# A twelve-layer latent transformer on one core: range clears, a key norm on two engines, early weights, and a new order of transfers in the 16-head layers

## What is computed

```python
x = x + L0_xattn(ctx, ln(x))   # 8 heads, ctx normalised row by row, rotary keys
x = x + L0_attn(ln(x));  x = x + L0_ffn(ln(x))
x = x + L1_xattn(ln(x), ctx)   # 16 heads of 16, mask per key
x = x + L1_attn(ln(x));  x = x + L1_ffn(ln(x))
x = x + L2_xattn(ln(x), ctx)   # 8 heads, cosine and variance terms
x = x + L2_attn(ln(x));  x = x + L2_ffn(ln(x))
x = x + L3_xattn(ln(x), ctx)   # 16 heads of 16, mask per query and key
x = x + L3_attn(ln(x));  x = x + L3_ffn(ln(x))
```

## Time and profile before

| | |
|---|---|
| median of 3 runs | 2720.01 us (2719.88 to 2721.12) |
| the profiled execution | 2719.54 us, its span 2717.6 us |
| mean granted clock of TensorE | 0.932 |
| busy: PE, PEld, DVE, ACT, POOL | 2356.9, 1462.9, 1794.6, 1238.8, 519.2 us |
| instructions | 58520 |

### The profile page before, as it was taken

The page is one execution under the profiler, slowest core; times in us unless marked ns, Lnnn a source line. Parts: engine busy times, 40 slices in busy tenths (PEclk is TensorE's granted clock), DMA queues, the critical chain, the costliest instruction groups (busy, mean ns, idle before and its releaser), DMA issues. The chain is left out here.

```text
span 2717.6 us, 58520 instructions
## 1 busy us (share of the span) xinstructions
PE 2356.9 (87%) x22114; PEld 1462.9 (54%) x22116; DVE 1794.6 (66%) x2945; ACT 1238.8 (46%) x2102; POOL 519.2 (19%) x297
## 2 busy tenths in 40 slices
PE   4699997999996585999997989999997449999978
PEld 3444434666564572666665745555555425555548
DVE  6466666888887617666662277777776767777721
ACT  6655554333332533777774233333332305555542
POOL 0255552000000002000000036555552010000000
PEclk8799998999998796999998999999998669999989
DMA  7677784565662448676673322222221057667554
GB/s 252 245 244 246 245 278 136 163 182 176 171 191 72 166 158 199 166 171 150 167 156 127 138 79 95 95 95 95 95 81 61 33 127 166 150 158 157 141 138 172
DMA packets 255993, 416.92 MB, mean 153 GB/s; under 512 B 32333, under 2 KB 217202, under 8 KB 255702
## 3 DMA queue, kind: packets, MB, share of 16 engines
q1 hardware_dynamic: 246902, 412.33, 52.4%
q10 hardware_dynamic: 8928, 2.23, 0.6%
HBM read 323.65 MB, written 90.85 MB: 153 GB/s over the span
## 5 line engine op out<-in xcount | busy, mean ns | idle before, releaser
L1493 DVE CUSTOM_DVE_ANT_0 l1x_junk<-l1x_pm,l1x_mrow,l1x_top 128x896 bf16<-128x896 f32 x224 | 247.1, 1148 | 112.7 <-PE l1x_pm L1649 112.6
L1493 DVE CUSTOM_DVE_ANT_0 l3x_junk<-l3x_pm,l3x_mrow,l3x_top 128x896 bf16<-128x896 f32 x224 | 246.1, 1147 | 88.7 <-PE l3x_pm L1649 88.2
L1577 ACT ACTIVATE l1x_prob<-l1x_ring,mask_col 128x512 f32<-128x512 f32 x392 | 248.1, 685 | 115.3 <-PE l1x_ring L1669 114.1
L1580 ACT ACTIVATE l3x_prob<-l3x_ring 128x512 f32<-128x512 f32 x392 | 213.2, 595 | 161.2 <-PE l3x_ring L1673 161.2
L2438 ACT ACTIVATE l2x_fsq<-l2x_f 128x1024 f32<-128x1024 f32 x98 | 103.5, 1057 | 276.6 <-DVE l2x_f L2326 276.6
L1068 ACT ACTIVATE l0x_att_pt<-l0x_att_pt 128x1024 f32<-128x1024 f32 x99 | 104.7, 1058 | 262.0 <-DVE l0x_att_pt L1007 262.0
L2610 POOL TENSOR_TENSOR l2x_gk<-l2x_f,l2x_ks 128x1024 f32<-128x1024 f32 x98 | 184.4, 1919 | 158.1 <-DVEq L2351 158.1
L1112 PE MATMUL l0x_att_pv<-l0x_wv,l0x_att_vin 128*128 128x512 f32 x392 | 194.4, 618 | 1.3 <-DVE l0x_att_tops L995 1.3
L2483 PE MATMUL l2x_kf<-l2w_w,l2x_nin 128*128 128x512 f32 x392 | 171.8, 598 | 4.3 <-DVE l2x_f L2326 3.8
L2483 PE MATMUL l2x_kf<-l2w_w,l2w_first 128*128 128x512 f32 x392 | 171.3, 597 | 0.0
L2326 DVE TENSOR_TENSOR l2x_f<-l2x_kf,l2w_bias 128x1024 f32<-128x1024 f32 x98 | 120.0, 1224 | 76.0 <-PE l2x_kf L2483 63.6
(11 more groups left out here) (695 smaller groups left out, 4836.3 us busy)
## 6 DMA issues: line engine op xcount, KB each, us to landing
l1x_kt<-scratch_KS SPq DMA_DIRECT2D x84, 448.0 KB, 9.2
l3x_kt<-scratch_KS SPq DMA_DIRECT2D x84, 448.0 KB, 8.8
scratch_KT<-l0x_max_kf SPq DMA_DIRECT2D x28, 896.0 KB, 7.0
l0x_att_kt<-scratch_KT SPq DMA_DIRECT2D x56, 448.0 KB, 7.1
scratch_KS<-l0x_side_kp SPq DMA_DIRECT2D x14, 1344.0 KB, 13.8
scratch_KS<-l2x_side_kp SPq DMA_DIRECT2D x14, 1344.0 KB, 5.8
l0fw_w<-L_ffn_exp_w SPq DMA_DIRECT2D x16, 1024.0 KB, 7.8
l1fw_w<-L_ffn_W SPq DMA_DIRECT2D x16, 1024.0 KB, 8.8
```

The costliest lines, as they stand in the source:

```text
L1493: dve.tensor_tensor_reduce(junk[x % 2][:, :, :], pm[x % 2][:, :, 0:SPLIT], mrow[b][:, :].rearrange("p (s k) -> p s k", s=2), 1.0, top[1 - ...
L1577: ins = act.activation(into, scores, ACT.Exp, bias=R.mask_col[:, bass.ds(m * TILES + n // 4, 1)])
L1580: ins = act.activation(into, scores, ACT.Exp)
```

## The change

- Semaphores are cleared by ranges of neighbouring numbers, dealt to SP, GpSimd, ScalarE and VectorE.
- Of the seven tiles of a chunk ScalarE scales five and VectorE two (tensor_scalar), in `factors`. In l0x chunk 0's statistics stand ahead of the wait for the vectors, and the pieces of other work move by one or two chunks.
- `AheadWeights` holds w_in of l0a and of l2a and all weights of l3a in a Stage of their own; they are loaded at the ends of l0x and l2x, and in l3x before the loop, and closed after l0f, l2a and l3f.
- In l1x and l3x the stack is loaded after the parts are in DRAM, and the values before. ScalarE loads only the first buffer of rows; the second is copied from the first by SP (`second_copy`). Two of the four query copies are on ScalarE, and TensorE begins after the first half.
- The spread, the products and the copy of `FoldedKeys` move from l1f to l1a; the scaling stays in l1f.

```diff
@@ Stage.__exit__
-            engines = (self.nc.gpsimd, self.nc.sync, self.nc.scalar, self.nc.vector, self.nc.tensor)
-            for n, s in enumerate(self.sems.values()):
-                engines[n % len(engines)].sem_clear(s)
+            engines = (self.nc.sync, self.nc.gpsimd, self.nc.scalar, self.nc.vector)
+            for n, numbers in enumerate(runs_of(s.num for s in self.sems.values())):
+                engines[n % len(engines)].sem_clear(numbers)
             self.nc.all_engine_barrier()
@@ KeyNorm.factors (DVE); scale (ACT) runs over range(self.BY_SCALAR), BY_SCALAR = 5
+        if m >= 2:
+            dve.wait_ge(self.sem("turned"), DC * (m - 1))
+        for t in range(self.BY_SCALAR, TILES):
+            last = dve.tensor_scalar(self.xn[m % 2][:, t, :], self.raw[m % self.DEPTH][:, t, :],
+                                     self.mv[m % 2][:, t, 0:1], self.rs[m % 2][:, t:t + 1], ALU.subtract, ALU.mult)
+        last.then_inc(self.sem("scaled_last"), 1)
@@ QueryRows
-        for rows in self.rows:
-            parts_to_rows(act, rows, self.scratch, PARTS_OF_Q, self.S.sem("q_in"))
+        parts_to_rows(act, self.rows[0], self.scratch, PARTS_OF_Q, self.S.sem("q_in"))
+    def second_copy(self, sp):
+        self.wait(sp)
+        sp.dma_start(self.rows[1][0:STACK], self.rows[0][0:STACK]).then_inc(self.S.sem("q_again"), 16)
@@ Heads16.run, SP
                     lead.sync(sp)
                     sp.wait_ge(S.sem("q_out"), 16)
+                    self.load_stack(sp, 0, 0)
+                    self.ones_rows(sp)
                     lead.later_sync(sp)
-                    self.ones_rows(sp)
+                    q.second_copy(sp)
                     top_to_rows(0, 0)
                     lead.last_sync(sp)
@@ Heads16.run, PE
-                    pe.wait_ge(S.sem("queries"), 1)
+                    pe.wait_ge(S.sem("queries"), 2)
                     for x in range(units):
+                        if x == units // 2:
+                            pe.wait_ge(S.sem("masked_q"), 2)
+                            pe.wait_ge(S.sem("queries_last"), 2)
                         max_unit(0, 0, x)
...
                     q.wait(pe)
+                    q.wait_second(pe)
@@ l1x Lead
-                heads.load_stack(sp, 0, 0)
+                self.late(sp.dma_start(w[:, 1, :, :], by_rows(A["L1_xattn_wv"])))
+                self.late(sp.dma_start(bv[:, :], A["L1_xattn_bv"].partition_broadcast(P)))
+                heads.load_values(sp, 0, 0)
@@ l3x Lead
-                heads.load_stack(sp, 0, 0)
+                heads.load_values(sp, 0, 0)
...
                 def last_sync(self, sp):
-                    pass
+                    R.ahead.load(sp)
@@ both Leads: masked_queries on DVE, turned_queries at the end of scalar
+        if c == 0:
+            dve.wait_ge(S.sem("masked_q"), 1)
+            dve.tensor_copy(qb_turned[c][0:64, :, :], qb[c][64:P, :, :]).then_inc(S.sem("queries"), 1)
+            dve.tensor_copy(qb_turned[c][64:P, :, :], qb[c][0:64, :, :]).then_inc(S.sem("queries"), 1)
+    act.wait_ge(S.sem("masked_q"), 2)
+    act.activation(qb_turned[1][0:64, :, :], qb[1][64:P, :, :], ACT.Copy).then_inc(S.sem("queries_last"), 1)
+    act.activation(qb_turned[1][64:P, :, :], qb[1][0:64, :, :], ACT.Copy).then_inc(S.sem("queries_last"), 1)
@@ l0a, l2a, PE (l3a the same)
-                pe.wait_ge(S.sem("w_in"), 16)
+                R.ahead.wait(pe)
@@ l1a, PE, after the last product of po and before the turn of xn
+                R.folded.tensor(pe, pa[:, 0:2, :])
                 turn_tensor(pe, S, "o", xn, pt, R.ident, ready="gated")
@@ l1f, PE
-                F.tensor(pe, ph[1])
                 turn_tensor(pe, S, "n", xn, pt, R.ident)
```

More of the change, by code:

```diff
@@ L31, with runs_of @@
 MASK_HEAD = MASK_ROW // 16
+def runs_of(numbers):
+    runs = []
+    for n in sorted(numbers):
+        if runs and runs[-1].stop == n:
+            runs[-1] = range(runs[-1].start, n + 1)
+        else:
+            runs.append(range(n, n + 1))
+    return runs
 class Stage:
@@ L259, in output, with __init__, load, tensors @@
         last.then_inc(S.sem("y"), 1)
+class AheadWeights:
+    def __init__(self, nc, name, parts):
+        self.S = Stage(nc, name)
+        self.buffers = [(self.S.sb(key, shape), pieces) for key, shape, pieces in parts]
+        self.loads = Loads(self.S.sem("loads"))
+    def load(self, sp):
+        for buffer, pieces in self.buffers:
+            for at, src in pieces:
+                self.loads(sp.dma_start(buffer[at], src))
+    def tensors(self):
+        return [buffer for buffer, _ in self.buffers]
+    def wait(self, eng):
+        eng.wait_ge(self.S.sem("loads"), self.loads.total)
+    def close(self):
+        self.S.__exit__(None, None, None)
 def l3_attn(nc, A, R):
@@ L274, in l3_attn @@
         pt, pqk, pv = S.psum("pt"), S.psum("pqk"), S.psum("pv")
-        loads = Loads(S.sem("weights"))
         block = S.nc.Block()
@@ L291, in _ @@
                 turn_vector(dve, S, "n", xT, pt)
-                dve.wait_ge(S.sem("weights"), loads.total)
+                R.ahead.wait(dve)
                 dve.wait_ge(S.sem("projected"), 1)
@@ L1945, in l0_xattn @@
     INNER = H * HD
+    R.ahead = AheadWeights(nc, "l0aw", [("w_in", [P, DC, 1024], [(slice(None), by_rows(A["L0_attn_W_in"]))])])
     with Stage(nc, "l0x") as S:
@@ L2191, in l2_xattn @@
     w, bias = folded.w, folded.bias
+    R.ahead = AheadWeights(nc, "l2aw", [("w_in", [P, DC, 1024], [(slice(None), by_rows(A["L2_attn_W_in"]))])])
     with Stage(nc, "l2x") as S:
@@ L2663, in mamba @@
     with Stage(nc, name) as S:
-        w_in = S.sb("w_in", [P, DC, 2 * INNER])
+        w_in, = R.ahead.tensors()
         w_out = S.sb("w_out", [P, IC, DIM])
@@ L2850, in l2_attn @@
                             "conv_b": "L2_attn_b_conv", "A_log": "L2_attn_A_log", "D": "L2_attn_D"}, True)
+    R.ahead.close()
+    R.folded.S.__exit__(None, None, None)
 class DecayWeights:
```

98 lines of the change are left out of this document (53 added, 45 removed).

## The result

The changed kernel takes **2707.68 us** (median of 5 runs, 2704.32 to 2710.64) against 2720.11 for the kernel before, run beside it (5 runs, 2719.88 to 2725.06). The ratio is 0.9946, 95% interval 0.9935 to 0.9957. It is faster, but by 12.4 us and not by 31: outside the range of the forecast.

A forecast was written before the change was run, and what follows sets the result against it. Twelve layers run one after the other, TensorE busy 87% of the span but waiting at their starts and ends. Gains 8.6 + 10.5 + 6.3 + 0.8 + 5.0 = 31.2 from 2719.5 give 2688.3, median 2689 us; range 2678 to 2700.

The forecast's parts named there:

- A: At the stage exits: clearing semaphores by range, with none on TensorE, gains 8.6 us (range 3 to 9.6).
- The other bound: At the stage exits: a clear might cost by its width, 0.05 us for each of some 470 semaphores.
- B and C: In l0x: earlier first statistics and the key norm split between ScalarE and VectorE gain 10.5 us (range 4 to 12.5).
- D: In l0a, l2a and l3a: first weights loaded a stage early gain 6.3 us (range 4 to 8).
- E: Folded pieces moved from l1f into TensorE's idle time in l1a gain 0.8 us (range -2 to 1.5).
- F: At the starts of l1x and l3x: new transfer order and shared query copies gain 5.0 us (range -2 to 12.4).
- the change does not do what it says: Rival, 0.08: in l1x and l3x the parts cross a queue that is not empty; l1x gains 0, l3x -3; 2696 us.
- Transfers share instead of queueing: Rival, 0.17: high parts move beside the stack and land in time; l1x gains 11.1, l3x 1.4; 2681 us.
- the forecast's own case: Main case, 0.53: 2683 to 2693 us; in l1x and l3x the high parts land behind stack and row loads.
- The slower rival, SP's serial chain: Rival, 0.04: in l1x and l3x parts, rows, second copy and tops follow each other; 18.8 us slower, 2738 us.

The follow-up runs named there:

- fourth: The changed kernel with all seven tiles of a chunk scaled by ScalarE again, l0x's earlier start kept: 2710.07 us, ratio 0.9962.
- fifth: The changed kernel with VectorE's piece of bias work in l0x one chunk later (m == 8, not 7): 2702.59 us, ratio 0.9928.
- third kernel: The kernel before the change with nothing but the semaphore clears by range: 2712.49 us, ratio 0.9973.
- seventh: The changed kernel with the second copy issued behind the first tops, and only the second chunk waiting for it: 2707.41 us, ratio 0.9939.
- ninth: The changed kernel, l1x and l3x first transfers issued without SP's wait, high parts and mask before stack, l0x bias work a chunk later: 2684.25 us.
- eleventh: The changed kernel with the folded pieces (spread, eight products, copy) back in l1f: 2709.85 us, ratio 0.9952.
- tenth: The changed kernel with six row loads of 256-byte pieces replaced by two of 4 KB pieces, same bytes, rows in wrong order: 2702.55 us.

## Why the prediction was right in sign and wrong in size

**A was right.** Forecast 8.6, the exits show 8.8, the clears alone 7.9 in the whole time. The other bound, a clear that costs 0.05 us for each semaphore, is excluded: the longest of the 53 took 0.28 us, the median 34 to 63 ns.

**B and C: the period was right, the stretch around it was not.** The forecast had the last factors at 85.6; they came at 91.39, 5.8 late. First, "a raw chunk lands in 4.9 us at best: the statistics can start at 9.2": the first chunk landed 7.2 us after its issue, and they started at 11.35, 2.15 late. The 4.9 came from a chunk in the loop, and at the stage's start three chunks and wq are issued within 1.8 us. Second, "3.3 for the one wait for TensorE's bias products, which stays": it grew to 5.50, for VectorE now arrives there earlier and TensorE does not. Two small waits, 0.82 for the queries and 0.67 for a raw chunk, were in no term. 2.2 + 2.2 + 0.8 + 0.7 = 5.9. VectorE's own work was sized well: 69.32 us busy against 69.8. The fourth and fifth runs show both sides: the start alone is given back to that wait, and when the wait is served a chunk later the last factors come 4.6 sooner.

**D was right in sum.** l3a gave 5.2, not 3.1. Its exit is still bound by SP's last expert load, as forecast:

```profile
2635.22 0.42 DVE L337 TENSOR_TENSOR tokens<-tokens,l3a_qk 128x256 f32<-128x256 f32 x1
2636.57 0.93 SPq L219 DMA_DIRECT2D l3fw_w<-L_ffn_W  x1
```

That load leaves the queue at 2637.50, 14.5 us into the layer, where it was 19.6: the 1.15 MB taken out of the stream were worth 5.1 us and not 3.1. l0a and l2a gave 1.2 and 0.9, not 1.5 and 1.7, and of l2a even that is not shown, for it took up to 75.3 us in other runs of the same code, against 74.5 before; there the wait for weights is gone, as forecast, and the turn of x stands in its place.

```profile
878.08 3.75 PE L2876 MATMUL l0a_pi<-l0a_xT,l0aw_w_in 128*128 128x128 f32 x16 [0.68 <-DVE l0a_xT L160]
...
2088.20 3.75 PE L2876 MATMUL l2a_pi<-l2a_xT,l2aw_w_in 128*128 128x128 f32 x16 [0.68 <-DVE l2a_xT L160]
```

**E agrees with the forecast, but is not shown**: 0.5 to 0.7 against 0.8, in layers that vary by more. The third kernel, in which the products still stand in l1f, has an l1a of 32.4 us (33.9 before, 32.5 with the change), so the 1.4 us of the table need not be E's. The folded products take 5.71 us in l1a instead of 5.15, and TensorE's wait of 5.20 there is gone: the turn follows them directly.

```profile
1482.23 5.71 PE L3265 MATMUL l1a_pa<-l2w_w,l2w_bb 128*128 128x512 f32 x8
1487.78 0.38 PE L154 MATMUL l1a_pt<-ident,l1a_xn 128*128 128x128 f32 x2
```

**F is the step that failed.** The forecast put it so: "the stack (12.5) and six row loads (3) follow together, to 1042.5; behind them the next chunk's high parts and mask row, each 448 KB: 1044.6 and 1046.7". From the stack's issue to VectorE's restart that is 20.7 us; it was 1044.33 - 1015.77 = 28.6. The rows took 20.2 (to 1035.94, when SP, which waits for them, issues the second copy) instead of 16.5, and high parts and mask row another 8.4 instead of 4.2. Both come from one assumption: that every transfer costs what its bytes cost at the stack's best rate. The row loads took longer beside the stack than "six, 3 us", and the last nine microseconds ran at 138 GB/s and not 210, which alone is 9 x (1 - 138/210) = 3.1 us. The forecast also had no term for the second copy's 384 KB, which move beside the high parts; the seventh run puts them at 0.15 us in l1x. And its own sum is not exact: 12.5 and 3 make 15.5 us, where it reckoned 16.5 in l1x and 15.8 in l3x. That the parts landed 14.8 us into the layer, a microsecond sooner than forecast, did not help.

For l3x the same term decides. The forecast had VectorE restart 1.1 us later than before; it restarts 9.4 later, and the layer is 8.9 longer. The two restarts account for 6.8 + 8.3 = 15.1 of the 17.9 us by which F missed; most of the rest is the clock in l1x (last section). The prediction saw that l3x had its high parts early and that the new order takes this away, but it priced the loss by the same sum. Before, the row loads never ran beside the stack, so no row priced the two together: the 3 us came from a stretch with other transfers. They were a guess within wide bounds, and the range for F, -2 to 12.4, held no case in which the sum was half as long again.

The experiments settle the mechanism. High parts ahead of the stack, and nothing else moved: 14 us back (second run). Stack ahead of SP's wait, and nothing else: 9 us back (eighth; 0.9946 - 0.9912 of 2720). No wait in SP's queue at all, with the second copy behind the tops and another place for the values: 19 us back (sixth). So two things lie in the new order: what VectorE needs first is issued last, and the issuing engine waits for a round trip of 2.4 us while 2.7 MB are still to be moved.

Of the rivals, "the change does not do what it says" gave the nearest sum (2696) for F at a loss, but by a mechanism that did not occur: it had the parts stuck behind the values, and they crossed in 2.4 us. "Transfers share instead of queueing" forecast the opposite for l1x. The Trainium skill ("DMA: Bandwidth & Descriptors", "Issuing engines are not separate DMA queues") says that transfers of all issuers run on the same 16 engines and interleave. Between SP's queue and ScalarE's the trace agrees: the row loads, issued beside the stack, took 5.6 to 16.4 us and landed along with it. Of transfers of one and the same issuer that sentence says nothing; in SP's queue the high parts came behind the stack, 15.4 us against 3.4, as in the forecast's own case. The slower rival, SP's serial chain, had the right place and the wrong link: the high parts were late and not the tops, and the two layers together lost 12.9 us and not 45.

## What to carry to other kernels

Order a DMA queue by who will stand still first, not by what is ready first: three transfers, 0.45 MB in all, that the bounding engine needs next landed in 3.4 us ahead of 2.7 MB and in 15.4 behind them. Don't put a wait for a round trip into the queue that issues the bulk; issue everything whose buffer is free, and let the small dependent transfers come last. Here the second rule was enough: once it was kept, the first brought nothing more (ninth run). And when an edit makes another engine the bound, list its waits for third parties: each that was hidden before counts in full, and grows by what the engine gained.

## What the runs showed of the chip that I had not expected

**The same code at another clock.** l2x was not edited, but it took 524.4 us before and 518.2 after. Its first three microseconds in the two kernels (granted clock, DMA share and GB/s are the last columns):

```profile
1574.10:1577.10 3.00, 2.74 (x4) 1.22 (x5) 2.22 (x12) 0.78 (x3) 0.00 (x0) 0.50 0.26 69
```

```profile
1566.50:1569.50 3.00, 2.70 (x7) 1.30 (x8) 2.22 (x12) 0.82 (x3) 0.00 (x0) 1.00 0.30 71
```

Before, TensorE began the layer at 1.2 GHz, after at 2.4. In the second, seventh and ninth experiments its first three microseconds had 0.72 to 0.79 and it took 521.3 to 521.6 us; in the third, fourth and eleventh 0.58 to 0.66, and 523.3 to 523.4; in the rest 1.00, and 518.1 to 518.2. So up to 6 us of this layer's length go with the clock that it begins at, which is nearly as large as D and larger than E. It is not the place of the folded products that sets it: the fourth has them in l1a, as the change has, and began at 0.66. Likewise in l1x: after the change the clock stays at 0.50 until 9.5 us behind the first group's start, where it rose 3.1 us behind it before, and from the first group on the layer is 3 us longer for the same work.

```profile
1059.00:1062.00 3.00, 3.00 (x24) 2.13 (x24) 1.13 (x4) 1.38 (x3) 0.00 (x0) 0.50 1.05 278
1062.00:1065.00 3.00, 3.00 (x53) 1.87 (x45) 0.99 (x1) 1.53 (x3) 0.00 (x0) 0.82 1.06 319
```

The seventh and the tenth run bear that out: their first groups started at 52.4 and 52.2 us into l1x, as with the change, but the clock was up some 7 us sooner, and l1x took 453.8 and 453.6 us and not 456.9. So some 3 of the 4.0 us that l1x lost are the clock's. What decides the moment of the rise was not tried.

**Busy is not fast.** The DMA share stands at 1.1 both where 210 GB/s are moved and where 138 are. A share near one says that the engines have work; how much they move has to be read beside it.
